# A fused two-layer transformer kernel: which of five PSUM work banks each step gets

## What is computed

```
x = x + attention0(layernorm(x))     # 16 heads, three attentions per head (latent keys, 64 picked tokens, window), gated and summed
x = x + ffn0(layernorm(x))           # square(relu(x @ W_fc)) @ W_proj = y, then five spiking steps:
                                     #   mem = 0.9*mem + y - reset;  spk = mem > 1;  the mean of spk is added
x = x + attention1(layernorm(x))     # 16 heads of width 16, rotary, causal
x = x + layernorm(x) @ sign(weight).T
```

## Time and profile before

| | |
|---|---|
| time, median of 3 runs | 3028.03 us (3027.3 to 3029.63) |
| the profiled execution, its own time | 3020.58 us |
| its span, first to last instruction | 3018.4 us |
| mean granted TensorE clock | 0.984 of full speed |
| TensorE busy | 2846.3 us, 94% of the span |
| VectorE busy | 1953.6 us, 65% |
| ScalarE busy | 1503.8 us, 50% |

### The profile page before, as it was taken

The page is one execution under the profiler, slowest core; times in us unless marked ns, Lnnn a source line. Parts: engine busy times, 40 slices in busy tenths (PEclk is TensorE's granted clock), DMA queues, the critical chain, the costliest instruction groups (busy, mean ns, idle before and its releaser), DMA issues. The chain is left out here.

```text
span 3018.4 us, 53728 instructions
## 1 busy us (share of the span) xinstructions
PE 2846.3 (94%) x18384; PEld 2030.1 (67%) x18384; DVE 1953.6 (65%) x6243; ACT 1503.8 (50%) x3228; POOL 961.6 (32%) x1764
## 2 busy tenths in 40 slices
PE   6999899999999999999999999999999999999977
PEld 4666676667766677666776667766677666776654
DVE  5666656775677656866567766667566776665644
ACT  2554344564445644465444664446544464445543
POOL 1233233432334313333133332334222332233332
PEclk7999999999999999999999999999999999999999
DMA  3110001000110011100101001110011000110000
GB/s 124 34 33 27 26 26 40 25 18 19 47 33 25 25 32 32 33 20 25 38 26 33 25 19 38 34 38 12 30 35 38 26 16 26 33 33 18 14 8 29
DMA packets 58701, 91.44 MB, mean 30 GB/s; under 512 B 19904, under 2 KB 32704, under 8 KB 58176
## 3 DMA queue, kind: packets, MB, share of 16 engines
q1 hardware_dynamic: 58432, 88.01, 9.9%
HBM read 81.68 MB, written 5.24 MB: 29 GB/s over the span
## 5 line engine op out<-in xcount | busy, mean ns | idle before, releaser
L1857 ACT ACTIVATE PR<-work 128x512 f32<-128x512 f32 (+1 forms) x1088 | 642.0, 598 | 710.4 <-PE work L1183 610.3
L1461 DVE CUSTOM_DVE_ANT_0 work<-work,KEEPB 128x128 f32<-128x128 f32 (+3 forms) x1536 | 667.3, 476 | 93.0 <-PE work L1147 92.3
L1972 POOL TENSOR_SCALAR_AFFINE_SELECT PR<-PR 128x256 f32<-128x256 f32 (+1 forms) x960 | 350.2, 370 | 724.5 <-ACT PR L1857 719.1
L1147 PE MATMUL work<-BIG 96*128 96x448 f32 (+8 forms) x1664 | 445.7, 356 | 25.2 <-DVE NMX L1461 10.8
L1181 PE MATMUL work<-BIG 99*128 99x512 f32 (+4 forms) x1152 | 423.8, 368 | 17.5 <-DVE BIG L1442 6.1
L1961 POOL TENSOR_TENSOR TOK<-AB 128x256 f32<-128x256 f32 (+1 forms) x320 | 219.0, 686 | 597.9 <-DVE AB L1423 544.3
L1218 PE MATMUL outs<-PR,ONES 128*32 128x512 f32 (+4 forms) x2304 | 404.8, 458 | 0.0
L1182 PE MATMUL work<-BIG 96*128 96x512 f32 (+4 forms) x1152 | 382.6, 332 | 0.0
L1183 PE MATMUL work<-BIG 96*128 96x512 f32 (+4 forms) x1152 | 380.9, 331 | 0.0
L1442 DVE TENSOR_TENSOR BIG<-work,BIG 96x512 fp32r<-96x512 f32 (+1 forms) x320 | 192.1, 603 | 289.0 <-ACT BIG L1742 288.7
L1147 PEld LDWEIGHTS work<-BIG 96*128 96x128 f32 (+1 forms) x1664 | 267.0, 192 | 157.5 <-issue 80.4
(11 more groups left out here) (185 smaller groups left out, 4641.9 us busy)
## 6 DMA issues: line engine op xcount, KB each, us to landing
NRM<-park SPq DMA_DIRECT2D x112, 192.0 KB, 3.1
WKW<-w_kw_dram SPq DMA_DIRECT2D x64, 256.0 KB, 2.7
WSEL<-w_sel_dram SPq DMA_DIRECT2D x64, 256.0 KB, 2.9
R<-park SPq DMA_DIRECT2D x72, 64.0 KB, 2.0
HN<-x_dram SPq DMA_DIRECT2D x8, 512.0 KB, 4.8
X<-x_dram SPq DMA_DIRECT2D x8, 512.0 KB, 4.0
out_dram<-X SPq DMA_DIRECT2D x7, 512.0 KB, 3.2
R<-park SPq DMA_DIRECT2D x16, 192.0 KB, 3.0
```

Source lines behind the costliest of these rows:

```text
L1147: last = mm(ps[:, col:col + n], q, k, start=(i_mm == 0), stop=(i_mm == len(u["mm"]) - 1))
L1461: last = v.tensor_tensor_reduce(ps[:, lo:hi], ps[:, lo:hi], KEEPB[:, T - (hi - lo):T], -1.0, -NEG, ALU.add, ALU.min, dst)
L1857: a.activation(PR[0:rows, j % NP, :], ps[0:rows, :], ACT.Exp).then_inc(exp_ready, 1)
L1972: gp.affine_select(blocks, blocks, [[0, len(cols)], [1, P]], ALU.is_ge, 0.0, base=0, channel_multiplier=-1).then_inc(exp_masked, 1)
```

## The change

The planner now keeps a clock. `now` is the time up to which TensorE's steps so far would take, and `until[k]` the time at which bank k is expected to have been read. A use gets, of the banks that are not held, the one with the smallest `max(until, now)`, and of equals the one that was used longest ago. What a use costs TensorE (`work`) and how long its readers need after it (`out`) stands in tables by kind of step. A held bank gets its `until` when it is released, at the same steps as before: 0.7 us after `now`. Steps that write no work bank (`pv`, the later parts of `y` and of the projections) move the clock on.

The tables `WORK_US`, `OUT_US`, `PIECE_US`, `STEP_US` and `VALUES_US` hold these numbers for 12 kinds of step. The core of the diff:

```diff
@@ -419,13 +419,16 @@
     def __init__(self, n):
-        self.n, self.uses, self.units, self.of, self.held = n, 0, 0, {}, set()
+        self.n, self.uses, self.units, self.of, self.held = n, 0, 0, {}, {}
         self.full, self.read, self.exp = [0] * n, [0] * n, [0] * n
-
-    def use(self, name, readers=1):
-        while self.uses % self.n in self.held:
-            self.uses += 1
-        k = self.uses % self.n
+        self.until, self.last, self.now = [0.0] * n, [-1] * n, 0.0
+
+    def use(self, name, readers=1, work=0.0, out=0.0):
+
+        k = min((k for k in range(self.n) if k not in self.held), key=lambda k: (max(self.until[k], self.now), self.last[k]))
+        self.now = max(self.now, self.until[k]) + work
+        self.until[k] = self.now + out
+        self.last[k] = self.uses
         self.uses += 1
         self.take(name, k, readers)
...
-    def hold(self, name):
-
-        self.use(name)
-        self.held.add(self.of[name][0])
+    def hold(self, name, work):
+
+        self.use(name, 1, work)
+        self.held[self.of[name][0]] = name
+
+    def release(self, name, out):
+
+        k = self.of[name][0]
+        del self.held[k]
+        self.until[k] = self.now + out
+
+
+WORK_US = {"unit": (0.85, 0.29), "max": (0.45, 0.29), "mt": (0.45, 0.45)}
+OUT_US = {"unit": 0.8, "max": 1.2, "mt": 1.3}
...
     def attention(layer, s):
         for x in STEPS[layer, s]:
             what, n = x[0:2]
             if what in ("unit", "max", "mt"):
-                work.use((s, layer) + x, {"unit": 0, "mt": 2}.get(what, 1))
+                work.use((s, layer) + x, {"unit": 0, "mt": 2}.get(what, 1), WORK_US[what][layer], OUT_US[what])
...
+            elif what == "pv":
+                work.now += VALUES_US[layer]
...
             elif what == "y" and x[3] == 0:
-                work.hold(("y", n, x[2]))
+                work.hold(("y", n, x[2]), 0.9)
+            elif what == "y":
+                work.now += 0.9
             elif what == "spike" and x[3] == 4:
-                work.held.discard(work.of["y", n, x[2]][0])
+                work.release(("y", n, x[2]), 0.7)
```

More of the change, by code:

```diff
@@ L441, in take @@
         self.of[name] = (k, free_at, self.full[k], self.read[k], exp_at)
-    def hold(self, name):
-        self.use(name)
-        self.held.add(self.of[name][0])
+    def hold(self, name, work):
[7 more added lines that the diff above has]
+OUT_US = {"unit": 0.8, "max": 1.2, "mt": 1.3}
+PIECE_US = {"qk": (1.25, 1.7), "sel": (0.9, 1.4), "nope": (0.45, 2.6), "val": (0.9, 1.3)}
+STEP_US = {"hT": (0.45, 0.8), "fc": (0.9, 0.8), "v": (0.9, 0.8), "sign": (0.9, 0.7), "qk": (0.9, 1.5)}
+VALUES_US = (1.2, 1.4)
 def plan_banks():
@@ L452, in piece @@
     def piece(g, m, what):
-        work.use((what, g, m), {"nope": 4, "val": 2}.get(PIECES[m][0], 3) if what == "piece" else 2)
+        kind = PIECES[m][0]
+        if what == "piece":
+            work.use((what, g, m), {"nope": 4, "val": 2}.get(kind, 3), *PIECE_US[kind])
+        else:
+            work.use((what, g, m), 2, 0.25 if kind == "sel" else 0.45, 1.4)
     def prologue(n, j):
@@ L457, in prologue, with held @@
                      ["pos"], ["selT"], ["imp"])[j]:
-            work.use(("pro", n, name))
+            work.use(("pro", n, name), 1, 1.7 if name == "imp" else 0.6, 1.0)
+    def held(what, n, i, x):
+        if x[0] in ("proj_early", "wo_early"):
+            work.hold((what, n, i), 1.3)
+        else:
+            work.release((what, n, i), 0.7)
     def attention(layer, s):
@@ L463, in attention @@
             if what in ("unit", "max", "mt"):
-                work.use((s, layer) + x, {"unit": 0, "mt": 2}.get(what, 1))
+                work.use((s, layer) + x, {"unit": 0, "mt": 2}.get(what, 1), WORK_US[what][layer], OUT_US[what])
             elif what in ("next_max", "next_mt"):
-                work.use((x[-1], 1, what[5:]) + x[1:-1], {"next_mt": 2}.get(what, 1))
+                work.use((x[-1], 1, what[5:]) + x[1:-1], {"next_mt": 2}.get(what, 1), WORK_US[what[5:]][1], OUT_US[what[5:]])
+            elif what == "pv":
+                work.now += VALUES_US[layer]
             elif what in ("piece", "piece_tr"):
@@ L469, in attention @@
             elif what == "kr":
-                work.use(x, 2)
+                work.use(x, 2, 0.25, 1.4)
             elif what == "pro_pe":
@@ L473, in attention @@
             elif what in ("hT", "fc", "v", "sign"):
-                work.use(x)
+                work.use(x, 1, *STEP_US[what])
             elif what in ("proj_early", "wo_early"):
                 for i in range(2):
-                    work.hold((what.split("_")[0], n, i))
+                    held(what.split("_")[0], n, i, x)
+            elif what in ("proj_last", "wo_last"):
+                work.now += 0.9
             elif what == "proj_add":
-                work.held.discard(work.of["proj", n, x[2]][0])
+                held("proj", n, x[2], x)
             elif what == "tail_add":
-                work.held.discard(work.of["wo", n, x[2]][0])
+                held("wo", n, x[2], x)
             elif what == "y" and x[3] == 0:
-                work.hold(("y", n, x[2]))
+                work.hold(("y", n, x[2]), 0.9)
+            elif what == "y":
+                work.now += 0.9
             elif what == "spike" and x[3] == 4:
-                work.held.discard(work.of["y", n, x[2]][0])
+                work.release(("y", n, x[2]), 0.7)
             elif what == "qk":
-                work.use(x, 2)
+                work.use(x, 2, *STEP_US[what])
             elif what == "heads":
                 for k in range(2):
-                    work.use(x + (k,), 2 - k)
+                    work.use(x + (k,), 2 - k, 0.5, 1.4 - 0.6 * k)
     attention(*BEGIN)
@@ L495, in plan_banks @@
     for x in TAIL_ORDER:
-        if x[0] == "wo_early":
+        if x[0] in ("wo_early", "tail_add"):
             for i in range(2):
-                work.hold(("wo", B - 1, i))
-        elif x[0] == "tail_add":
-            work.held.discard(work.of["wo", B - 1, x[1]][0])
+                if x[0] == "wo_early" or i == x[1]:
+                    held("wo", B - 1, i, x)
         elif x[0] in ("hT", "sign"):
-            work.use((x[0], B - 1) + x[1:])
+            work.use((x[0], B - 1) + x[1:], 1, *STEP_US[x[0]])
     return work
```

## The result

The changed kernel takes 3036.7 us (median of 8 runs, 3034.9 to 3038.29), before 3028.83 us; the ratio is 1.003, 95% interval 1.0021 to 1.004: slower by 6 to 12 us. The profiled execution took 3036.22 us, its span is 3034.0.

What follows compares the result with a forecast made beforehand. TensorE, busy 2846.3 us of 3018.4, was taken to set the time. The terms -2.7 - 0.7 - 0.7 + 2.6 + 2.0 = +0.5 us on 3020.58, carried over to the median 3028.03, gave 3028.5 us, range 3020 to 3037.

Steps and rivals of the forecast that it cites:

- Where the change acts: 219 uses get another predecessor; six spike waits move to `nope`, and the 2.76 us wait before a `max` goes.
- The closing `y`, 2.7 us: Pass (1, 6): `max` no longer waits 2.76 us, `mt` starts 2.3 us earlier, 0.4 us of clock back: 2.7 us gained.
- The second closing `y`, 0: The `unit` at 2889.54 loses its 2.02 us wait, but transposes behind wait for DVE: 0 gained, at most 2.0.
- The first `y`, 0.7: Pass (0, 1): the `max` at 427.57 loses its wait of 0.72 us: 0.7 us gained.
- The second layer, 0.7: Seven passes lose waits at `unit` (0.37 us) and `mt` (0.45 us); a quarter of the second kept: 0.7 gained, at most 5.7.
- Between 0 and 5.2 I take half, 2.6: First layer's six passes: `nope` waits for `y`, `qk` comes 0.86 us later; partly caught up at DVE's maxima: 2.6 us lost.
- second rival: Same: the first layer's loss is caught up and no more is gained, -4.1, 3023.9 us; chance 0.25.
- I take two of the six and 1.0 us each: 2.0: Stalls of some 1.9 us at `nope` in six first-layer passes halve the clock: 2.0 us lost, bounds 0 and 10.2.
- the third one: Slower: stalls at `nope` in passes (0, 2) to (0, 7) cost 0.86 us and a half-clock stretch each, 3039.3 us; chance 0.15.

Runs made afterwards that it cites:

- experiment 1: Kernel before with strict turns, but in passes (0, 2) to (0, 7) `nope` trades banks with the `qk` piece behind it, getting the bank of `y`: 3035.98 us, ratio 1.003.
- experiment 2: Changed kernel, but `nope` of passes (0, 2) to (0, 7) may not take the bank of `y`; the `qk` piece takes it as before: 3024.61 us, 0.9994.
- 4: Kernel before, but in pass (1, 6) `max` (7, 3) and the `mt` behind it trade banks, so the `mt` gets the closing `y`'s: 3024.53 us, 0.9992.
- 12: Kernel before with two bank trades: closing `y`'s bank to the `mt` in pass (1, 6), first `y`'s to `max` (3, 3) in pass (0, 1): 3022.96 us, 0.9993.
- 15: Repeat, for its trace, of the kernel before with `nope` taking the bank of `y` at six places: 3035.9 us, ratio 1.0041.
- 7: Kernel before, but at the six places the `qk` piece and the `piece_tr` behind it trade banks, removing the wait for `y`: 3026.49 us, 0.9998.
- 9: Kernel before with DVE's statistics of the second `y` half (`var`) moved behind the `piece_tr` that follows the `sel` piece: 3036.42 us, 1.0034.
- 10: Kernel before with the `qk` piece and `piece_tr` trading banks at the six places, and `var` behind the `piece_tr` after the `sel` piece: 3037.21 us, 1.004.
- 13: Kernel before with `qk` piece and `piece_tr` trading banks at the six places, and `var` put ahead of DVE's gap: 3023.57 us, 0.9997.
- 5: Changed kernel with one filler product of 0.86 us ahead of each of the six `nope` products: 3030.69 us, ratio to before 1.0016.
- 3: Changed kernel with two filler products, about 0.86 us each, ahead of each of the six `nope` products: 3031.95 us, ratio to before 1.0014.
- 6: Kernel before with one filler product of 0.86 us at the six places, ahead of the `qk` piece that waits for `y`: 3027.91 us, 1.0005.

## Why the prediction was wrong

The time lies just inside the range, but I gave "the same" 0.69 and "slower" 0.17.

*Where the change acts* was right: six waits at `nope`, a free `max` at the closing `y`, nothing else that matters (experiments 1 and 2).

*The closing `y`, 2.7 us.* Measured 2.90 to 2.96 by 2892.9, in the place and by the steps forecast: the `mt` waits 1.61 us, forecast 1.3, and takes 0.60 us again. What I didn't have is that the clock takes part of it back. Difference to before since 2860, us:

```
                    at 2892.9  at 2900  at 3015
the change              -2.90    +0.07    -1.81
2   undone at six       -2.91    -1.08    -0.45
4   closing alone       -2.95    -1.37    -0.01
12  two gains           -2.96    -2.96    -2.40
```

The waits near the end lie otherwise, and a half-clock stretch meets other work. The first window is of the change, the second of before:

```profile
2908.30:2915.10 6.80, 6.10 (x17) 2.76 (x18) 1.69 (x5) 1.76 (x3) 0.00 (x0) 0.51 0.01 1
2906.70:2913.40 6.70, 2.80 (x13) 2.80 (x14) 1.13 (x2) 2.98 (x8) 3.60 (x11) 0.50 0.00 0
```

In the change TensorE is busy for 6.10 us of such a stretch, before for 2.80. This is seen in one trace of each. The ratios of 2 and 4 say 1.8 and 2.4 us gained, 2.1 and 0.5 short of what their places sum up to, which their intervals can't tell from nothing.

*The second closing `y`, 0.* Right: the wait before the `unit` is gone, and TensorE stands 3.18 us for DVE behind it, before 0.32.

*The first `y`, 0.7.* Measured 1.0: `max` and what follows stay that much earlier, up to 650 us in the change's trace.

*The second layer, 0.7.* Measured 0. The `mt` is 0.63 us earlier and three products on, at 1013.44, TensorE waits 0.58 us for DVE's maxima. It was the right mechanism; a quarter was too much.

*"Between 0 and 5.2 I take half, 2.6."* This is the step that failed. Measured 0.82 x 6 = 4.9. My reason was that the later wait of 0.91 us for DVE's maxima would shrink. It stands at 0.90, before 0.91. DVE's way to those maxima starts at a product of TensorE's own. DVE's row in the change, then in before:

```profile
968.56 0.69 DVE L1721 CAST BIG<-work 128x512 fp32r<-128x512 f32 x1 [0.73 <-PE work L1333]
...
965.49 0.69 DVE L1690 CAST BIG<-work 128x512 fp32r<-128x512 f32 x1 [0.74 <-PE work L1302]
```

DVE waits for that product and then works without another wait up to the maxima, 7.35 us to TensorE's row at 975.91, before 7.37. So they come as late as TensorE does. The prediction had this in its second rival, as "against it", and gave it no weight in the sum. A wait can give time back only if its cause doesn't move along.

*"I take two of the six and 1.0 us each: 2.0."* The second failure, in size. A fall costs 2.45 - 0.8 = 1.65 us, since TensorE has work all through the stretch; I had 1.7 as the bound and took 1.0 without a row for it. And 11 of 18 fell, so 3.67 of six on average: 6.05 us. With these two, the six places cost 4.9 + 6.05 = 11.0 us, against the 10.9 us that lie between experiment 2 and the change; experiments 1 and 15, the six places alone, measured 9.1 and 12.4. So close an agreement is partly luck. Of this, fillers gave back 4.8 and 4.2 us, the clock's part. The sum with what was measured, -1.8 - 1.0 + 0 + 4.9 + 6.05, is about +8 us where I had +0.5.

*The rivals.* It became the third one, the longer stall that costs the clock, at 0.15. I had it decide "once more than four of the six" fall, and that was a slip in the sum: by its own terms -4.1 + 5.2 + 3 x 1.7 = 6.2 us, above the bound of 6.1 with three falls already. Counted rightly, it deserved more than 0.15.

The page "TensorE: Matmul & The Clock Gate" of the Trainium skill, section "A second HAM failure mode: psum-queue depth-cycling", describes a kernel whose clock goes up and down because TensorE stands idle between groups of products as it goes through its PSUM banks. These traces agree that idle time at a bank can cost the clock: 1.65 us a fall, behind 11 of 18 stalls.

Why the mirror of the loss gave nothing: two chains start at the reading of `y` and meet at the `sel` piece. TensorE's own was as long as DVE's to within 0.1 us: with TensorE's freed the `sel` piece came 0.08 us sooner behind `nope`, with DVE's shortened 0.03 us. Lengthening TensorE's costs in full; shortening it alone gives 0.00; both shortened give 0.45 (experiments 7, 9, 10, 13). What is left open is how DVE's chain would go on past ACT's copy of `nope`, and which stalls of 1.76 us cost the clock.

## What to carry to other kernels

A planner of buffers that goes by expected times is as good as its weakest number. Here that was 0.7 us for a read that ended 1.86 us after TensorE came for `nope`: it moved six waits to a worse instruction, and 2.5 undid the loss. Before counting on a later wait to absorb a delay, ask whether what it waits for is itself made by the delayed engine. And a stall has two prices, its length and the clock behind it; a product of no use, put into the stall, tells them apart.

## What the hardware showed that I had not expected

A wait of 1.76 us was followed by a stretch of 3.4 us at 1.2 GHz in 11 of 18 cases, with the same instructions and nearly the same times around it, and only partly at the same places from one execution to the next. In all eleven the lower clock began 0.5 to 1.4 us after the wait's end. A wait of 0.90 us at the same spot, behind `nope` or ahead of it, was followed by none in 36 (the traces of before and of 2, 4, 5, 9 and 12), and a wait filled with products by none in 12 (3 and 6). So the cost of such a stall has to be taken as an average over executions; a single profile, as mine of before at 3020.58 us against a median near 3028, can lie 8 us off, mostly by the clock: it was granted 0.984 in that execution. Of the 29 of the same kernel that experiment 1 was held against, the fastest, 3021.18 us, had the highest clock, 0.983, and the slowest, 3029.96 us, the lowest, 0.978.
